# Linear attention on quarters and halves of the matrix array, without its zero-state products, and local x loads issued earlier

## The reference, cut to what matters

```
def _phi(x, proj): return jax.nn.elu(x @ proj) + 1.0
h = _ln(x, g1, beta1)                                   # h2 = 16 heads of 64
q = _phi((h @ wq).reshape(b, s, H, DH), proj)
k = _phi((h @ wk).reshape(b, s, H, DH), proj)
v = (h @ wv).reshape(b, s, H, DH)
def step(carry, qkv_t):                                 # over the 1024 rows of one batch
    kv, ksum = carry                                    # both start at zero for each batch
    kv = kv + k_t[..., :, None] * v_t[..., None, :]
    ksum = ksum + k_t
    num = jnp.einsum('bhd,bhde->bhe', q_t, kv)
    den = jnp.einsum('bhd,bhd->bh', q_t, ksum) + 1e-06
    return ((kv, ksum), num / den[..., None])
x = x + outs @ wo
```

## Time and profile before

| | before |
|---|---|
| median of three | 3473.15 us |
| profiled execution, its own time | 3473.36 us |
| its span | 3471.5 us |
| TensorE matmul busy | 3236.5 us, 93% |
| VectorE / ScalarE / GpSimd busy | 2384.9 / 1554.4 / 1730.9 us |
| linear attention, first to last turn | 1067 to 1795 us |
| one of its turns | 22.85 us |
| window stages | from 2039.6 and from 2757.4 us |

### The profile page before, as it was taken

How to read it: one execution, slowest core, us unless ns; L and a number is a source line. 1 busy time by engine, 2 the same in 40 slices (tenths; PEclk the granted TensorE clock), 3 DMA queues, 4 the chain that set the end, 5 groups by cost and what they waited for, 6 DMA issues and landing times. The chain is left out here.

```text
span 3471.5 us, 67759 instructions
## 1 busy us (share of the span) xinstructions
PE 3236.5 (93%) x25216; PEld 2348.8 (68%) x25216; DVE 2384.9 (69%) x5183; ACT 1554.4 (45%) x3124; POOL 1730.9 (50%) x2205
## 2 busy tenths in 40 slices
PE   7888888888778999999999989999899999999999
PEld 5666667666557888888876656666666566666565
DVE  7999999999765565655654457777633377777332
ACT  6877788776342222222221135555411255555111
POOL 6988898888561000000012247777611277777221
PEclk9999999999889999999999999999999999999999
DMA  4011011110261000010012221111111111121210
GB/s 146 1 64 64 12 53 64 64 58 23 87 208 41 14 14 12 12 38 14 14 47 73 70 65 39 39 53 47 50 58 47 64 32 38 38 76 30 73 62 30
DMA packets 167004, 176.52 MB, mean 51 GB/s; under 512 B 22756, under 2 KB 150264, under 8 KB 166296
## 3 DMA queue, kind: packets, MB, share of 16 engines
q1 hardware_dynamic: 163272, 162.81, 14.6%
q0 software_dynamic: 3408, 9.38, 0.7%
HBM read 94.06 MB, written 78.09 MB: 50 GB/s over the span
## 5 line engine op out<-in xcount | busy, mean ns | idle before, releaser
L3125 ACT ACTIVATE win_probs<-win_sc,win_nbias,tile_rn 128x256 f32<-128x256 f32 (+1 forms) x512 | 275.5, 547 | 293.4 <-DVE win_nbias L3214 293.3
L438 POOL TENSOR_TENSOR ssm_acc<-ssm_acc,ssm_weighted 128x512 f32<-128x512 f32 x255 | 339.3, 1341 | 101.6 <-ACT ssm_weighted L587 101.2
L424 POOL TENSOR_SCALAR ssm_ub<-ssm_uT,ssm_bcT 128x512 f32<-128x512 f32 x512 | 359.2, 726 | 25.0 <-PE ssm_pu L1151 21.2
L1151 PEld LDWEIGHTS ssm_pu<-ident,ssm_ub 128*128 128x128 f32 x2048 | 239.4, 143 | 183.9 <-issue 87.2
L3321 PE MATMUL win_pa<-win_w_wqkv,tile_hT 128*128 128x512 f32 x744 | 361.4, 623 | 0.0
L1151 PE MATMUL ssm_pu<-ident,ssm_ub 128*128 128x128 f32 x2048 | 310.0, 280 | 50.4 <-DVE ssm_state L821 33.3
L1167 PE MATMUL ssm_pt<-ident,ssm_state 128*128 128x128 f32 x2040 | 278.6, 278 | 48.4 <-DVE ssm_acc L831 30.4
L821 DVE TENSOR_TENSOR_SCAN ssm_state<-ssm_da,ssm_carry,ssm_pu 128x512 f32<-128x512 f32 x256 | 312.4, 1261 | 3.0 <-ACT ssm_da L575 3.0
L2000 POOL TENSOR_TENSOR lin_rstd<-lin_mv,lin_eps 128x1 f32<-128x1 f32 x30 | 5.7, 192 | 611.0 <-DVE lin_mv L173 611.0
L2712 PE MATMUL glu_up<-block_hT,glu_w_w 128*128 128x512 f32 x704 | 305.7, 592 | 3.4 <-DVEq L88 3.4
L821 DVE TENSOR_TENSOR_SCAN ssm_state<-ssm_da,ssm_pu 128x512 f32<-128x512 f32 x256 | 296.8, 1200 | 5.4 <-PE ssm_pu L1151 2.7
(11 more groups left out here) (429 smaller groups left out, 7077.9 us busy)
## 6 DMA issues: line engine op xcount, KB each, us to landing
sorted_rows<-block_zeros SPq DMA_DIRECT2D x8, 4290.0 KB, 15.7
block_wide<-x SPq DMA_DIRECT2D x18, 512.0 KB, 6.6
tile_raw<-in_tables SPq DMA_DIRECT2D x64, 128.0 KB, 2.2
a<-tile_y SPq DMA_DIRECT2D x64, 128.0 KB, 1.7
block_wide<-a SPq DMA_DIRECT2D x32, 256.0 KB, 3.3
block_x<-a SPq DMA_DIRECT2D x16, 512.0 KB, 5.5
block_x<-sorted_rows SPq DMA_DIRECT2D x39, 130.0 KB, 2.7
x<-block_more SPq DMA_DIRECT2D x16, 256.0 KB, 2.1
```

The lines of the kernel that those rows point to most:

```text
L424: nc.gpsimd.tensor_scalar(ub[:, i % 2, t, :], uT[:, k % 2, t, :], bcT[:, k % 2, t, n:n + 1], 1.0, ALU.mult, ALU.mult).then_inc(ub_ready.se ...
L438: nc.gpsimd.tensor_tensor(acc[:, k % 2, t, :], acc[:, k % 2, t, :], weighted[:, j, :], ALU.add)\
L1151: last = nc.tensor.transpose(pu[c][:, t * P:(t + 1) * P], ub[:, i % 2, t, c * P:(c + 1) * P], ident)
L3125: nc.scalar.activation(probs[:, head, keys_seen(turn)], sc[j][:, r, keys_seen(turn)], ACT.Exp, bias=nbias[:, g, j, r:r + 1], scale=rn[:, t ...
```

## The change

1. Turned keys and turned attention are no longer transposes of 128x128. Each pair becomes four products of 64x64 (64 rows, 64 columns of the array) with a 64-column piece of the identity: 32 products in place of eight transposes. `pb[0]` now takes the first head of each pair and `pb[1]` the second (for attention: the first and the second 64 queries), so both banks are complete only at the end of the group.
2. Scores: each 64x128 product is cut by keys into two quarters. The quarter of the later 64 keys leaves out the earlier 64 queries, except in tile 0.
3. Projection: each 128x128 product is cut into two column halves, 64 in place of 32.
4. The state's products are left out in the four tiles that open a batch; turned keys, `k_rows`, phi(k)^T v and the update are left out in the four that close one. `keep` goes, with its loads and waits; ScalarE's copy to `k_rows` has no per-row factor.
5. Window stages: the loads of tiles 2 and 3 are issued before the wait for `pending` and before the MLP's weights.

```diff
+                for g in range(2 if not closes(turn.i) else 0):
+                    act.wait_ge(kt_ready.sem, kt_ready.at(kept_until(turn.i), g + 1))
                     nc.scalar.activation(
-                        k_rows[:, g * GP:(g + 1) * GP, :], pb[g][:, :].rearrange("p (r d) -> p r d", d=P), ACT.Copy,
-                        scale=keep[:, turn.side, :]).then_inc(k_rows_ready.sem, 1)
+                        k_rows[:, :, HALVES[g]], pb[g][:, :].rearrange("p (r d) -> p r d", d=DH), ACT.Copy)\
+                        .then_inc(k_rows_ready.sem, 1)
...
                         for k in range(KD):
-                            last = nc.tensor.matmul(feature_banks[g][:, r * P:(r + 1) * P], wqk[:, g // 2, k, cols],
-                                                    hT[:, k, :], start=(k == 0), stop=(k == KD - 1))
+                            for half in HALVES:
+                                last = nc.tensor.matmul(feature_banks[g][half, r * P:(r + 1) * P],
+                                                        wqk[:, g // 2, k, at + half.start:at + half.stop], hT[:, k, :],
+                                                        start=(k == 0), stop=(k == KD - 1), skip_group_check=True)
...
                 for a in range(GP):
-                    for j in range(2):
-                        half = slice(j * DH, (j + 1) * DH)
-                        ins = nc.tensor.matmul(score_banks[2 * g + j][:, a * P:(a + 1) * P],
-                                               qkT[half, side, 1, g * GP + a, :],
-                                               qkT[half, side, 0, g * GP + a, :], start=True, stop=True)
+                    for keys in reversed(HALVES):
+                        seen = slice(keys.start if i else 0, P)
+                        for j, half in enumerate(HALVES):
+                            ins = nc.tensor.matmul(score_banks[2 * g + j][keys, a * P + seen.start:(a + 1) * P],
+                                                   qkT[half, side, 1, g * GP + a, keys],
+                                                   qkT[half, side, 0, g * GP + a, seen], start=True, stop=True,
...
-                for g in range(2):
-                    pe.wait_ge(attnT_ready.sem, attnT_ready.at(i - 1, g + 1))
-                    for r in range(GP):
-                        last = nc.tensor.transpose(pb[g][:, r * P:(r + 1) * P], qkT[:, side, 1, g * GP + r, :], ident)
-                    last.then_inc(kt_ready.sem, 1)
+                pe.wait_ge(attnT_ready.sem, attnT_ready.at(i - 1))
+                for r in range(PR if not closes(i) else 0):
+                    for keys in HALVES:
+                        for j, half in enumerate(HALVES):
+                            last = nc.tensor.matmul(pb[j][keys, r * DH:(r + 1) * DH], qkT[half, side, 1, r, keys],
+                                                    ident[half, half], start=True, stop=True, skip_group_check=True)
+                            if r == PR - 1 and keys == HALVES[1]:
+                                last.then_inc(kt_ready.sem, 1)
...
-                for r in range(LAST):
+                for r in range(LAST if not opens(i) else 0):
...
+                if not closes(i):
+                    pe.wait_ge(k_rows_ready.sem, k_rows_ready.at(kept_until(i)))
+                    pe.wait_ge(attn_ready.sem, attn_ready.at(i, 2))
...
+                pe.wait_ge(scores_ready.sem, scores_ready.at(i))
+                for r in range(PR):
+                    for j, half in enumerate(HALVES):
+                        for g, queries in enumerate(HALVES):
+                            last = nc.tensor.matmul(pb[g][half, r * DH:(r + 1) * DH], attn[queries, 2 * r + j, :],
+                                                    ident[queries, queries], start=True, stop=True, skip_group_check=True)
...
+            for side in range(2):
+                sp.wait_ge(tp_ready.sem, tp_ready.at(side))
+                sp.wait_ge(table_ready.sem, table_ready.at(side))
+                start(Turn(1, side), load(Turn(1, side)))
             for sem, total in pending:
                 sp.wait_ge(sem, total)
             upcoming.load(sp)
```

122 lines of the change are left out of this document (56 added, 66 removed).

## The result

| | before | after | ratio (95%) |
|---|---|---|---|
| median of 13 runs each, us | 3471.45 (3463.67 to 3478.16) | 3482.78 (3474.85 to 3484.64) | 1.0029 (1.0021 to 1.0037) |
| profiled execution, own time | 3473.36 | 3479.88 | |
| its span | 3471.5 | 3477.9 | |

The account below looks back on a forecast made before the run. TensorE's own instruction time was taken to bound linear attention. Linear attention +3.5 us and windows -3.0 on 3473.36 gave 3473.9; set against the median, 3473.7 us was predicted, range 3462 to 3485.

Parts of the forecast that it names:

- The bound: Linear attention: a turn costs TensorE's own instructions, 22.85 us; only TensorE's time counts until another engine becomes late.
- Turned keys, turned attention, projection: Ordinary turn, TensorE's groups: turned keys +0.34 us, turned attention +0.24, projection -0.21.
- Scores and the wait for `k_rows`: Ordinary turn: scores by quarters -0.12 us; wait for ScalarE's copies ahead of the scores' second group +0.10.
- Rival C: Linear attention: the waits don't come, `k_rows` costs nothing, opening and closing tiles wait less; 3465.3 us, chance 0.12.
- rival D: Scores: the two halves of the keys run less freely, 13% slower; 3481 us, or 3503 one after another; chance 0.22.
- rival E: Projection: weights of column halves load in the open, +3.2 us a turn; 3573 us, chance 0.03.
- turned keys leave 0.87 and add nothing: Tiles closing a batch: dropping the turned keys saves their 0.87 us and brings no added quarter cost.
- Opening turns: Tiles opening a batch: VectorE's second large division holds phi(k)^T v, so leaving out state products gains only 0.17 us each.
- nothing in sum but the keys' 0.87: Tile 31, the last: earlier turned attention brings nothing, as the output product waits for ScalarE's copies; only 0.87 us saved.
- The windows: Both window stage starts: early loads shorten waits for `tile_raw` and half clock, together -3.0 us.
- I take it that it shrinks to the other's length: Second window stage: half clock of 10.23 us shrinks to the first stage's 6.83, worth -1.3 us.
- Rival B: Window starts: half-clock stretches disappear and both waits count in full; -12.3 us, 3464, chance 0.18.

Follow-up runs that it names:

- c_twice: The changed kernel with the turned keys' quarter products made twice in a row; a single run, 3518.8 us.
- c_plain: The changed kernel with turned keys by plain full-array products with the identity; a single run, 3493.4 us.
- a_keys: The changed kernel with turned keys again by eight 128x128 transposes; ratio 0.9989 to the kernel before.
- a_both: The changed kernel with turned keys and turned attention both again by transposes; ratio 0.9964 to the kernel before.
- b_order: a_both with the transposes of `n` put between the two halves of the scores in closing turns; ratio 0.9950 to the kernel before.
- b_proj: a_both with the projection again by full-array 128x128 products; ratio 0.9977 to the kernel before.
- b_zero: a_both with the left-out zero-state products and closing tiles' key products put back; ratio 0.9976 to the kernel before.
- a_winlate: The changed kernel with the early window loads put back behind the wait and the weights; ratio 1.0031 to the kernel before.
- e_seen: a_both with the scores' quarters computing all 128 queries, no column left out; ratio 0.9965 to the kernel before.

## Why the forecast was nearly right, and what was wrong in it

- **The bound** (TensorE alone, everything else covered) held in the ordinary turns: there the changes of its groups give the 0.43. In the tiles that open and close a batch it stands still for VectorE, 5.5 us more in sum than before; the forecast had most of these waits, and missed one.
- **Turned keys, turned attention, projection**: +0.38, +0.26, -0.20 against +0.34, +0.24, -0.21. Right, and shown by the runs that undo each: the quarters' 16 rounds of 0.058 us and the changes of form are in c_twice, the two records of a product against the one of a transpose in c_plain. The rest of the 0.08 a turn is in the scores (0.02), where the wait ate the whole gain. In 24 turns it makes 1.9 us.
- **Scores and the wait for `k_rows`**: -0.10 and +0.10 against -0.12 and +0.10. Right. Rival C's free `k_rows` is refuted by a_keys (the 0.10 goes with the quarters), rival D by the 1.90 of a_both, and rival E by the projection's 7.14.
- **The step that failed first** is that of the tiles that close a batch: "turned keys leave 0.87 and add nothing". They had covered the residual's reading of `lin_pt`, and each closing turn got a wait of 0.66. I had looked at what the keys cost and at what waits for their result, and not at what ran beside them. Cost against the forecast: 1.61 - 0.85 = 0.76, three times, 2.3 us. b_order shows it. The other half of that step was better than forecast: the wait ahead of the turned attention was 0.24, not 0.3 to 0.4.
- **Opening turns**: I had -0.17, to be added to the ordinary difference of +0.35, which is +0.18 against a turn before. Three came out at -0.07 and turn 0 at -0.18, together 1.1 us better than forecast. phi(k)^T v starts 15.24 us into the turn, before 15.67. Before, VectorE stood still for 0.50 us between the two statistics instructions, and in the changed kernel for 0.15; why that gap shrank was not tried. The wait ahead of phi(k)^T v was 0.77 us, where I had 0.8 to 1.1.
- **The last turn**: "nothing in sum but the keys' 0.87", which with scores and attention is -0.75. It came out at +0.42, since a stretch of half clock of 3.41 us fell on its output product (5.26 us for 3.72). In a_both there is no half clock in this place, and from the last `n` to the MLP it takes 38.2 us (before 40.1, after 40.7). Without the 1.5 us by which the output product is longer, the last turn would stand at about -1.1. So the forecast was 1.2 us off by something that differs from kernel to kernel: of after and the twelve experiments nine have such a stretch there, and four (a_both, b_proj, b_zero, b_order) have none.
- **The windows**: -3.0 forecast, -0.9 measured, a miss of 2.1 us. The term that failed is "I take it that it shrinks to the other's length": the half clock did not become shorter when the longest gap did. Its length stayed at 10.24 us, and the gaps moved to GpSimd's `win_probs` and to ScalarE's and VectorE's `win_probsT`, so that L3378 is reached 0.36 us earlier than before. a_winlate, with the loads late, has 23.43 us to that group, so the loads account for 0.12 of it, where I had 1.3 for the copy that comes sooner. Rival B (half clock gone, -12.3) is refuted as well. Even the -0.9 is not shown to be the work of the loads. In the second stage a_winlate has it without them. In the first, the kernels that load early take from 466.71 (b_proj) to 468.46 (a_keys), and the 468.16 of before lies inside. The half clock can be shorter with the same loads: b_proj, b_zero and b_order have 6.83 us at the second stage's start. b_proj and b_zero take 466.70 and 466.69 for that stage, so the shorter stretch is worth some 0.4 us when it comes, where I had 1.3. b_order takes 469.21, with a wait of 1.31 us for `tile_raw` later in the stage and a longer half clock near its end. Why the stretch is 6.83 in one kernel and 10.24 in another was not found.
- **The sum**: against the forecast of +0.5 us, ordinary turns are +1.9, closing ones +2.3, opening ones with turn 0 -1.1, the last +1.2, before's own wait in turn 12 -0.3 and the windows +2.1. That makes +6.6; the spans differ by 6.4. None of them is large; most of them fell to one side, and I had written that my bounds would not. The last turn and the windows, 3.3 us of it, hang in good part on where half clock fell in one profiled execution of each kernel; had they come out as forecast, that would have been luck too. The medians differ by 11.3 us and the ratio's interval is 7.3 to 12.8; what is above 6.5 has no cause in any stage of the two profiles and stays open, as said at the start. And the forecast gave 0.45 to no change beyond 0.2%: the time lies in its range, but what came is the slower outcome, by 0.29%.

## What to carry to other kernels

Before a small piece of work is taken out of a full engine's queue, look at what it covered: read which bank the next instruction writes and who still reads it; here 0.66 of the 0.87 us came back as a wait. Before float32 work is split over array quarters, count the records of what it replaces: here quarters beat the plain product (1.09 us against 1.78) and lost to the transpose, which is one record a block and cost 0.47 us less a turn, wait included. The longest wait at a stage's start can be worth nothing: here, with other engines' work right behind it and half clock behind that, its removal changed the stage from 467.14 to 467.15 us. And before a difference of a stage is put down to an edit, look at the granted clock of that stage in every kernel on record: here two kernels with the same window code, after and a_keys, differ by 1.0 us in it.

## What was not expected of the hardware

- The quartered products over 64 columns go out at four records in 0.058 us (64 more records in 0.93 us, c_twice). With 64 records more a turn, "issue" gaps of up to 0.6 us appear in some turns, which the changed kernel does not have in its ordinary turns.
- Quarters of unequal column counts do not help each other: 1.91 us for the scores with half of the columns left out in one half of the keys, and 1.91 with all of them (e_seen).
- Column halves of the array load weights beside each other's products at no visible cost: 0.11 us a round of two for 128 columns, 7.14 us for 64 rounds (after and a_both; 7.34 for the full array in b_proj).
- In the last turn a stretch of half clock of 3.41 us came in e_seen behind waits of 1.6 (for `lin_attn`) and 0.7 us (for `block_yn`), and stayed away in b_order behind longer ones, 2.2 and 0.7. The sum of the waits alone does not decide it. Where the half clock falls also differs between kernels whose code is the same there: at the start of the first window stage 6.83 us in after and 10.24 in a_keys, at that of the second 10.24 in a_both and 6.83 in b_zero.
